# Layers stage: selection counts, thresholds and picks one slot earlier, and the last batch masked in one slot

## What is computed

```python
h = jnp.einsum('blv,dv->bld', x, Win) + bin
def body(h, p):
    y = silu(layernorm(h, l1w, l1b)); y = sconv(y, phz, lc)      # decaying complex scan
    h = h + y * scl
    y = silu(einsum('bld,fd->blf', layernorm(h, l2w, l2b), w1) + b1_)
    return (h + einsum('blf,df->bld', y, w2) + b2_, None)
...
_, topk_idx = jax.lax.top_k(cm, k)          # k = 154 of 256 entries of each context column
mask = zeros.at[b_idx, l_idx, topk_idx].set(1.0)
...
out = einsum('bseo,bse->bso', expert_out, w_e)   # two experts of eight for each row
```

## Time and profile before

| | us |
|---|---|
| median of 3 runs (1160.13 to 1164.36) | 1164.08 |
| profiled execution, its own time | 1166.08 |
| its span, first to last instruction | 1164.0 |
| layers stage with the selection, slots 1 to 19 | about 112 to 420 |
| gated context and routing | about 420 to 650 |
| expert matmuls | about 650 to 1164 |
| PE busy over the span | 1056.5 (91%) |
| DVE, POOL, ACT busy over the span | 564.1, 493.5, 402.8 |

### The profile page before, as it was taken

How to read it: one execution, slowest core, us unless ns; L and a number is a source line. 1 busy time by engine, 2 the same in 40 slices (tenths; PEclk the granted TensorE clock), 3 DMA queues, 4 the chain that set the end, 5 groups by cost and what they waited for, 6 DMA issues and landing times. The chain is left out here.

```text
span 1164.0 us, 13959 instructions
## 1 busy us (share of the span) xinstructions
PE 1056.5 (91%) x3739; PEld 584.2 (50%) x3740; DVE 564.1 (48%) x1655; ACT 402.8 (35%) x1142; POOL 493.5 (42%) x662
## 2 busy tenths in 40 slices
PE   6787889999999879789992999999999999999995
PEld 6785455555545435336992444444444444444442
DVE  5646578888787868988847211111111121111111
ACT  2435787787776317757720000000000000000000
POOL 3833567667575100006702533444433334444331
PEclk9878899999999889988555999999999999999998
DMA  7310111110000232002686337373735536373332
GB/s 302 134 55 0 47 46 37 44 48 1 1 1 1 73 145 73 1 1 91 260 318 239 87 72 216 72 223 83 230 77 149 139 74 214 75 226 86 81 73 37
DMA packets 38465, 120.29 MB, mean 103 GB/s; under 512 B 6220, under 2 KB 9351, under 8 KB 38408
## 3 DMA queue, kind: packets, MB, share of 16 engines
q1 hardware_dynamic: 25592, 79.77, 18.6%
q0 software_dynamic: 12816, 39.86, 15.7%
HBM read 82.91 MB, written 36.70 MB: 103 GB/s over the span
## 5 line engine op out<-in xcount | busy, mean ns | idle before, releaser
L1985 PE MATMUL bank<-T,X 128*128 x1184 | 509.9, 594 | 2.9 <-DVE X L2029 2.9
L1985 PEld LDWEIGHTS bank<-T,X 128*128 128x128 f32 x1184 | 225.5, 191 | 286.7 <-issue 286.7
L2043 DVE TENSOR_SCALAR X<-bank,col_p 128x512 f32<-128x512 f32 x37 | 27.8, 751 | 401.9 <-PE bank L1985 401.9
L2009 ACT ACTIVATE X<-bank,col_p 128x512 f32<-128x512 f32 x37 | 25.4, 687 | 504.8 <-PE bank L1985 504.8
L1938 POOL DMA_INDIRECT X<-x_nrm,col_s x156 | 150.0, 962 | 75.8 <-issue 46.9
L1947 POOL DMA_INDIRECT out_dram<-X,col_d x37 | 60.0, 1621 | 264.8 <-DVE X L2043 251.1
L449 POOL TENSOR_TENSOR T<-T 128x8 f32<-128x8 f32 x216 | 93.3, 432 | 16.3
L822 ACT ACTIVATE M<-X,T 128x256 bf16<-128x256 f32 x200 | 98.5, 498 | 0.0
L458 POOL TENSOR_TENSOR rs<-ve,neg_half 128x4 f32<-128x4 f32 x36 | 45.7, 1270 | 91.1 <-DVE ve L961 90.9
L634 PE MATMUL bank<-nat,T 128*128 128x512 f32 x128 | 69.4, 672 | 7.9 <-ACT X L810 5.4
L216 POOL TENSOR_TENSOR late<-late,neg_half 128x1 f32<-128x1 f32 x32 | 17.5, 546 | 125.7 <-DVE late L212 125.7
(11 more groups left out here) (330 smaller groups left out, 1529.0 us busy)
## 6 DMA issues: line engine op xcount, KB each, us to landing
T<-in_L_ffn_expert_w_dram SPq DMA_DIRECT2D x8, 4096.0 KB, 17.7
out_dram<-X SPq DMA_DIRECT2D x17, 512.0 KB
M<-in_x_dram SPq DMA_DIRECT2D x16, 512.0 KB, 7.4
X<-in_x_dram SPq DMA_DIRECT2D x16, 512.0 KB, 5.2
x_nrm<-H SPq DMA_DIRECT2D x16, 512.0 KB, 3.6
T<-in_ctx_dram SPq DMA_DIRECT2D x9, 512.0 KB, 3.6
X<-x_nrm,col_s POOLq DMA_INDIRECT x156, 3.7
X<-in_ctx_dram SPq DMA_DIRECT2D x4, 512.0 KB, 7.1
```

The costliest lines, as they stand in the source:

```text
L1985: mm = nc.tensor.matmul(bank[2 * u + n][:, :], xgt[u][:, k, :], Tf[:, ds(odd * D + (k * N + n * BANK), BANK)], start=(k == 0), stop=(k == ...
```

## The change

The whole selection behind `means` comes one slot sooner. POOL computes `first_thresholds` at the head of an even slot, `other_end` and `last_threshold` in the even slot behind the second `power` and in front of `turn_in`, and `third_threshold` in the odd slot in the same place. ACT counts low in the slot of the first thresholds, high in the next, third and last in the two that follow. DVE takes `without_under`, `greatest`, `taken` and `pick` one slot sooner and masks one slot sooner; of the last batch both halves are masked in one slot, so the loop has two slots fewer. `split_bias` moves from slot 2 to slot 1, since `w` is now written in slot 2. No instruction is added or removed.

```diff
-        SLOTS_END = FIRST + 2 * B + 9
+        SLOTS_END = FIRST + 2 * B + 7
+        def masking(s):
+            b, h = divmod(s - FIRST - 8, 2)
+            return [] if not 0 <= b < B else [(b, 0), (b, 1)] if b == B - 1 else [(b, h)]
...
                     if 0 <= s + 2 < FINAL:
                         power(s + 2, ve1, rt1)
-                    if s > 0 and starts(s, 4) is not None:
-                        third_threshold(starts(s, 4))
-                    if starts(s, 5) is not None:
-                        other_end(starts(s, 5))
-                        last_threshold(starts(s, 5))
+                    if s >= 0 and starts(s, 2) is not None:
+                        first_thresholds(starts(s, 2))
                     if 0 <= s + 1 < VISITS:
                         turn_out(s + 1)
                     if 0 <= s < VISITS:
                         power(s, ve2, rt2)
+                    if starts(s, 4) is not None:
+                        other_end(starts(s, 4))
+                        last_threshold(starts(s, 4))
+                    if s > 0 and starts(s, 3) is not None:
+                        third_threshold(starts(s, 3))
                     if 0 <= s + 2 < VISITS:
                         turn_in(s + 2)
-                    if s == 0:
-                        third_threshold(0)
-                    if starts(s, 2) is not None:
+                    if s < 0 and starts(s, 2) is not None:
                         first_thresholds(starts(s, 2))
+                    if s < 0 and starts(s, 3) is not None:
+                        third_threshold(starts(s, 3))
...
+                        if starts(s, 2) is not None:
+                            count_low(starts(s, 2), 0, KD)
                         if starts(s, 3) is not None:
-                            count_low(starts(s, 3), 0, KD)
+                            count_high(starts(s, 3), 0, KD)
                         continue
                     if s == 0:
                         act.wait_ge(h_mid, s + 1)
                         square(s, sq2)
-                        count_high(0, 0, KD)
+                        count_third(0, 0, KD)
                         silu(s + 2)
                         copies(b0, 2 * h0)
                         copies(b0, 2 * h0 + 1)
-                        count_third(0, 0, KD)
+                        count_low(1, 0, KD)
                         continue
...
                     if starts(s, 3) is not None:
-                        count_low(starts(s, 3), 0, KD)
-                    if starts(s, 6) is not None:
-                        count_last(starts(s, 6), 0, KD)
+                        count_high(starts(s, 3), 0, KD)
+                    if starts(s, 4) is not None:
+                        count_third(starts(s, 4), 0, KD)
...
-                    if b9 is not None:
-                        mask(b9, h9)
+                    for b, h in masking(s):
+                        mask(b, h)
                     if 0 <= s < VISITS:
                         plus_eps(s, False, var2, ve2)
-                    if b7 is not None:
-                        taken(b7, h7)
+                    if b6 is not None:
+                        taken(b6, h6)
...
-                    if s == 2:
+                    if s == 1:
                         split_bias()
```

## The result

The changed kernel takes 1170.32 us (median of 20 runs, 1162.75 to 1174.69), beside 1161.70 us of the kernel before (20 runs). The ratio is 1.0059, with a 95% interval of 1.0043 to 1.0075: some 7 us slower (the two medians lie 8.6 us apart). The forecast was 1173.6 with a range of 1161 to 1180, and slower as the likeliest sign.

What follows compares the result with a forecast made beforehand. PE and DVE were taken to set the pace; -1.1 (end) + 2.0 (start) + 6.2 (`split_bias`) + 2.4 (steady slots) = +9.5 us on the median of 1164.08 gave 1173.6 us, range 1161 to 1180.

Steps and rivals of the forecast that it cites:

- `split_bias` (+6.2): Slots 2 and 3: `split_bias` delays `middle(2)`; slot 2 +7.4, slot 3 -2.8, half clock +1.6; bounds +2.5 to +9.
- The 1.6 for the stretch at half clock: Slot 2: PE idles some 4 us twice, so the clock dips there, costing 1.6 us.
- from that variance on PE's own 9.0 us to the next slot are unchanged: Slot 2: behind the variance matmul PE still takes 9.0 us to the next slot.
- The start (+2.0): Slots -2 to 1: ACT's wait goes, an equally long chain through POOL, PE, ACT replaces it; +2.0, bounds -5.1 to +4.
- The queue of POOL in front of `power(2)`: Start: `third_threshold(0)`, 5.68 us, stands in front of `power` of visit 2's first norm, which ends at 109.8.
- The rival "faster": Start: ACT's 5.06 us wait before `hidden(0)` goes and nothing replaces it; -8.0, 1156 us; chance 0.12.
- The steady slots (+2.4): Slots 5 to 15: odd slots' `scan` waits for POOL's late `turn_in`, even slots gain; +2.4, bounds -2.5 to +4.
- The end (-1.1): End of the stage: PE's check matmul no longer waits for DVE, 0.8, plus 0.25 in slot 16; -1.1, bounds -1.5 to nothing.
- The signs: Changed profile: `split_bias` ends 9 us after slot 2's first `hidden`; slot 2 near 27, 3 17.4, 8 16.1, 9 18.9.
- The base: Whole kernel: the sum was added to the median of 1164.08 us, not the profiled 1166.08, giving 1173.6.

Runs made afterwards that it cites:

- e12: The changed kernel measured once more, with no edit: 1169.87 us, ratio 1.0047 to the kernel before.
- e11: The kernel before measured once more, with no edit: 1163.73 us, ratio to itself 0.9987.
- e2: The kernel before with only `split_bias` moved, from the end of slot 2 to slot -1 behind `scan(0)`: 1162.15 us, ratio 0.9981.
- e3: The kernel before with only `split_bias` moved from the end of slot 2 to the end of slot 1: 1165.74 us, ratio 1.0015.
- e1: The changed kernel with `split_bias` in slot -1 behind `scan(0)` instead of at the end of slot 1: 1166.11 us, ratio 1.0016.
- e8: The changed kernel with ten more DVE operations between the last mask and the check value: 1166.24 us, ratio 1.0016.
- e4: e1 with POOL's start reordered: `third_threshold(0)` behind `power(2)`, `first_thresholds(1)` behind the `power` of slot 0's second norm: 1160.47 us, ratio 0.9974.
- e10: e6 with two more DVE operations of 0.41 us in `taps(1)` at the end of slot 1: 1156.99 us, ratio 0.9945.
- e5: The changed kernel with POOL's `turn_in` ahead of the chain of 14 and `third_threshold` instead of behind them: 1167.55 us, ratio 1.0028.
- e9: e6 with `split_bias` back at the end of slot 1: 1160.69 us, ratio 0.9965.
- e6: e4 with e5's POOL order added, `turn_in` ahead of the long chains: 1156.40 us, ratio 0.9939.

## Why the prediction was right, and where it was off

The sign, the range and the main cause hold: the change costs 6 to 7 us, and slot 2 is where. The forecast of +9.5 was 2.6 too high, and part of its closeness is luck, as said below. Term by term, from the second pair (e12 less e11):

| term | forecast | measured |
|---|---|---|
| start, to slot 2 | +2.0 | +0.9 (-0.1 between the means of four profiles each: before, e2, e3, e11 and after, e1, e8, e12) |
| slot 2 | +9.0 | +8.5 |
| slot 3 | -2.8 | -2.8 |
| slots 4 to 15 | +2.4 | +1.6 |
| slot 16 to the check matmul | -1.1 | -1.3 |
| sum | +9.5 | +6.9 |

- **`split_bias` (+6.2).** Right in size (slots 2 and 3 together +5.7) and in cause: of slot 2's +8.5 it makes 6.66 (e3). PE's two waits in slot 2 were 5.45 and 1.35 us, where I had some 4 twice. Inside the term two errors cancel. The 1.6 for the stretch at half clock is not there: the stretch came, but ahead of the variance, where PE waited for DVE anyway, and the step "from that variance on PE's own 9.0 us to the next slot are unchanged" holds (9.05). And `middle` moved out by 9.2 us, not by 8.3, since `taps` takes 4.77 us beside POOL's `turn_in`, which now comes late behind a chain of nine (137.30 in after); I had looked at no price for that. That the clock can cost 1.3 to 3.0 us behind the variance is shown by e1, e4 and e10, in kernels where PE had not just waited 5 us.
- **The start (+2.0).** The queue of POOL in front of `power(2)` is real, and mending it brings 1.9 us (e4). `hidden` on ACT came at 121.97 (forecast 122.7), 1.87 us later than before (1.48 counted from `scan(0)`). What failed is the step from there to slot 2, where I passed the shift on whole. Before, PE had waited 5.39 us for ACT and then ran its passes at half clock, 3.78 us for four; in after it has no such wait there, and it is through with both mixing passes at the same time (L632 at 124.57, before L625 at 124.39, and 1.02 instead of 1.52 us). From 118.87 to 122.50 the granted clock is 0.50, from there to 124.57 it is 0.92, where the last four passes fall. The clock that a removed wait gives back was left out of the sum. The rival "faster" named the same wait, and it failed for the reason given against it: the new chain took its place.

```profile
118.87 5.87 PE L641 MATMUL bank<-nat,T 128*128 128x512 f32 x8
124.57 1.02 PE L632 MATMUL bank<-X,T 128*128 128x512 f32 x2
```

- **The steady slots (+2.4).** The mechanism is shown (`scan` waits for `turn_in`; e5 takes the wait away and slot 9 falls from 18.27 to 17.91). Mis-sized is its price: slots 5, 9 and 13 grew by 0.21, 0.49 and 0.94 us where I had 1.0, 1.1 and 2.4, since the chain took 6.38 us where I took the slowest row, 7.42. The even slots 8 and 12 gave back 0.40 and 0.83, where I had 0.7 and 1.2. Slots 14 and 15 came to +0.2 together (-0.81 and +1.03), where I had -0.2. Unforeseen are slots 6 and 10 (+0.31 each) and 7 and 11 (+0.15 each). The slots that I had priced sum to +0.6, so +1.6 against +2.4 is luck in part. The Trainium skill (GPSIMD Engine Reference, Key points) says that POOL shares its SBUF interfaces with VectorE, with contention for VectorE instructions that have two inputs in SBUF. The rows of after agree: the same 14 operations take 5.31 us in slots 2, 6 and 10, where DVE runs a maximum, a match_replace and `scale` beside them, none with two inputs in SBUF, and 5.96 to 6.38 in slots 4, 8, 12 and 14, where `without_under` with its two inputs is among them; beside an idle DVE they took 5.29 in slot 1 of before (121.23).
- **The end (-1.1).** As forecast PE's check matmul no longer waits for DVE, which is through 5.9 us earlier; e8 shows at the check matmul that this slack is real, so it buys nothing. The size is not shown: this stretch takes 32.7 to 35.3 us from one kernel to another with the same code in it (e1, e4).

```profile
423.55 0.28 PE L793 MATMUL bank<-T,ones 128*128 128x1 f32 x2
```

- **The signs.** `split_bias` ends 9.1 us after `hidden`'s first matmul (9 forecast), slot 2 27.15 (27), slot 3 17.41 (17.4), slot 8 16.48 (16.1), slot 9 18.27 (18.9).
- **The base.** I took the median of three runs, 1164.08; that of twenty was 1161.70. The 2.4 us between them are more than the error of any one term.

## What to carry to other kernels

Work that has slack belongs where its engine idles, and not one slot earlier at the end of a full queue: the same twelve operations cost nothing in slot -1, 2.8 us at the end of slot 2 (e2) and 4.3 to 7.3 us at the end of slot 1 (slot 2 of after against e1, of e9 against e6; 6.7 of e3 against e2). On an in-order engine ask of each operation that is moved which short operation, with its input ready, will stand behind it; with the two short ones of POOL (`power`, `turn_in`) put first the change that cost 6 us became a gain of 7 (e6 with `split_bias` in slot -1; by its own place `split_bias` is 2.8 of that in the kernel before too). And where PE is nearly full, a wait is priced with its clock: look whether the rows behind it are at the faster or the slower duration, and whether another wait stands behind them: in e1 half clock made 3.0 us of the slot, in after, ahead of a second wait, nothing.

## What the runs showed of the hardware that I had not expected

- **A turn on POOL slows DVE at its side.** Beside a 128x512 `turn_in` six scalar_tensor_tensor operations took 4.77 us instead of 3.89; in slot -1 of e1 a 128x1024 subtraction with two inputs took 2.06 us beside POOL's `turn_out`, and 1.23 us in slot 1 of e9 (138.73), where POOL stood idle. A chain of 128x8 operations beside it did not slow `taps` (3.89 us in e6):

```profile
88.04 2.06 DVE L1042 TENSOR_TENSOR T<-late,T 128x1024 f32<-128x1024 f32 x1 [0.15 <-DVE T L1040]
```

```profile
87.48 1.53 POOL L471 TENSOR_TENSOR X<-X,T 128x512 f32<-128x512 f32 x1 [3.21 <-DVE X L957]
```

- **A short wait can cost the clock, or not.** In slot 2 PE's waits of 0.52 (before) and 1.10 us (e6) left the granted clock at 2.4 GHz; behind 1.65 (e1), 1.98 (e4) and 2.01 us (e10) it fell to 1.2 GHz. But it stayed up behind 1.35 (after) and 1.62 us (e9), where it had just come back from a longer stretch at 1.2 GHz. The length of the wait alone doesn't decide, and neither does it set the price: behind 1.98 (e4) and 2.01 us (e10) half clock made 3.0 and 1.3 us of the slot.
- **The spread between runs of one kernel has places.** Up to 3.3 us lie ahead of `scan(0)`, 1.4 us in a slot that falls to half clock in one execution and not in another, and up to 7 us in the stage behind the layers, with its granted clock (738.2 to 745.4 us, 0.60 to 0.70). A difference of a few us between two profiles is not the change's until these are taken out.
